# Softmax denominators of the attention stage: block transposes and sums on VectorE with two 16-column products, in place of two 512-column products

## The chip, the cores and the metric

The kernel runs on one core of a Trainium2 chip. A core has TensorE (PE in the rows; its weight loads are shown apart, as PEld), VectorE (DVE), ScalarE (ACT), GpSimd (POOL) and SyncE (SP, which issues most DMAs). Each engine runs its own instructions strictly in order, and engines wait for each other through semaphores. The metric is the device time of one execution in microseconds; lower is better.

## The reference

A block of four residual layers on x of 4 sequences x 1024 tokens x 256 features: a head-mixing layer, an expert layer (8 experts, 256 tokens of each sequence for each), causal attention with 16 heads of 64, and the expert layer again. The change lies in the attention:

```python
q = einsum('ntc,hdc->nhtd', x_q, w_q)        # likewise k, v
a = einsum('nhtd,nhsd->nhts', q, k) / sqrt(64)
a = where(causal_forbidden, -inf, a)
a = softmax(a, axis=3)                        # exp(a - max) / sum over s
y = einsum('nhts,nhsd->nthd', a, v).reshape(n, t, -1)
return y @ w_o
```

The changed part computes the sum over s for each head and query, takes its reciprocal, and brings it into the layout in which the values' product is multiplied by it.

## The kernel before

**Stages by time.** Head mixing and the first expert layer fill the span up to about 605 us, the attention runs to about 1800 us (its first unit overlaps the end of the first expert layer), and the second expert layer takes the rest.

**Units, chunks, pairs.** Attention is done in 32 units: 4 sequences x 8 head pairs, the two heads of a pair side by side in every tile. A unit has two chunks of 512 queries. Chunk 0 uses key blocks 0 to 3 (of 128 keys), chunk 1 key blocks 0 to 7. Key blocks go two at a time, so a unit has 6 such steps: two for chunk 0 and four for chunk 1. A step writes scores with keys on the partitions (L1423, L1439), ScalarE takes the exponential into a tile t_p of 128 keys x 2 heads x 512 queries (L1734), GpSimd masks the diagonal blocks (L2410) and adds the tiles of a chunk into t_acc (L2427, L2430), and TensorE multiplies the values by t_p into bank 6 (L1458, `weigh`). ScalarE copies the finished chunk to t_pvs (L1752).

**Denominators.** t_acc holds sums over key blocks; the sum over its 128 partitions is still to be taken. `divide` does it on TensorE (L1468): for each head a product of 64 columns of ones with 512 columns of t_acc, which leaves the sum repeated on 64 partitions. `sum_rows` on VectorE transposes the bank in 32x32 blocks (L2239) and takes the reciprocal of one column of 32 (L2241); `scale_rows` transposes back a 32-fold repeated copy (L2248) into t_den; GpSimd multiplies t_pvs by it into t_yT (L2444), from which the output product L1483 is made.

**Maxima of the next unit.** While a unit is attended, TensorE makes score rows of the next one (L1388, 512 columns; L1401, 128 or 256 columns) and VectorE takes their maxima (L2215 with the mask, always followed by a read of the accumulator, and L2221). After the last of them TensorE turns the 16x128 maxima (L1410, `max_rows`), VectorE negates them (L2230, t_neg), and a DMA moves them into a row of t_qb. The first score product L1439 of the next unit waits for that DMA. TensorE also makes the projections of the unit after (L1360, L1374), whose rests VectorE takes (L2199, L2185).

**What sets the order.** A hand-written set of Python generators, run once per engine. `attend` gives 24 places per unit, and the loop of `units` hangs the other work on places by number. `finish(n)`, run after the scores of step n, issues `divide` of a chunk three steps after its last pair started, then the weigh of the step before, then `sum_rows`, and `scale_rows` one step later. Seven banks of PSUM (0 to 5 and 7) are handed out in rotation, in TensorE's order, to scores, maxima, projections and denominators. A bank can be written again only when its reader has drained it, so the taker of a bank waits for the reader of whatever took it seven takes before.

## Time and profile before

| | |
|---|---|
| median of 3 runs | 2219.75 us (2218.33 to 2220.87) |
| the profiled execution | 2221.76 us, its span 2220.0 us |
| TensorE busy | 2142.3 us (97%) |
| VectorE busy | 1463.3 us (66%) |
| GpSimd busy | 1374.8 us (62%) |
| ScalarE busy | 1002.8 us (45%) |
| granted TensorE clock, mean | 0.989 |
| chain that ended last | TensorE 74%, VectorE 8%, GpSimd 4%, issue 3% |

The span runs from the first to the last instruction. The busy share of TensorE counts the time in which at least one matmul is in flight, and the starts of matmuls that follow each other without a wait are closer together than their durations, since they are pipelined. So what a group of matmuls costs is read as the distance from its first start to the start of the next group. The times at the left of the timeline rows below are such starts.

### The profile page before, as it was taken

How to read it: one execution, taken by the hardware profiler on the slowest of the kernel's cores; microseconds unless marked ns; L12 is line 12 of the kernel's file. 1: busy time of each engine (PE TensorE's matmuls, PEld its weight loads, DVE VectorE, ACT ScalarE, POOL GpSimd, SP SyncE). 2: the span in 40 equal slices, each digit the busy share in tenths (PEclk: the TensorE clock that was granted, in tenths of full speed). 3: DMA queues.
4: the chain of work that ended last, by engine and by line, in shares of the span. 5: the costliest groups of instructions: out<-in, count | busy, mean ns of one | idle time of the engine just before them, and what ended most of it. 6: DMA issues, size and time to landing. Idle time of an engine off the chain costs nothing.

```text
span 2220.0 us, 34078 instructions
## 1 busy us (share of the span) xinstructions
PE 2142.3 (97%) x12130; PEld 1597.7 (72%) x12130; DVE 1463.3 (66%) x3344; ACT 1002.8 (45%) x1908; POOL 1374.8 (62%) x1242
## 2 busy tenths in 40 slices
PE   7998999999999999999999999999999999999997
PEld 5446888889876666766667666567666588899997
DVE  7375687776757666476775577874876646975553
ACT  6302543454355555255553355542555425444442
POOL 4313675777357676466664566663777846777774
PEclk9999999999999999999999999999999899999999
DMA  4524554555432221221222132222221245545552
GB/s 133 185 95 127 140 134 103 142 141 134 98 92 58 58 58 49 67 77 51 75 70 74 39 86 50 56 67 64 61 77 30 67 135 130 139 111 132 136 143 29
DMA packets 145048, 206.04 MB, mean 93 GB/s; under 512 B 19432, under 2 KB 112112, under 8 KB 144880
## 3 DMA queue, kind: packets, MB, share of 16 engines
q1 hardware_dynamic: 120304, 170.30, 25.7%
q0 software_dynamic: 24576, 33.57, 9.1%
q8 instruction: 97, 1.59, 0.3%
q14 instruction: 71, 0.58, 0.1%
HBM read 130.03 MB, written 39.85 MB: 77 GB/s over the span
## 4 chain that ended last, share of the span: by engine, by line
PE 74%; DVE 8%; POOL 4%; issue 3%; ACT 2%; DMA 1%; SPq 1%; POOLq 0%; DVEq 0%; ACTq 0%
PE psum L1311 12%; PE psum L1332 11%; PE psum L1458 11%; PE psum L1360 8%; PE psum L1423 7%; PE psum L1439 6%; PE psum L1483 5%; PE psum L1374 4%; PE psum L1388 3%; PE psum L1468 3%; POOL t_acc L2430 2%; DVE f_hlo L2169 1%; DVE f_hhi L2167 1%; PE psum L1401 1%; PE psum L1279 1%
## 5 line engine op out<-in xcount | busy, mean ns | idle before, releaser
L1734 ACT ACTIVATE t_p<-psum 128x512 f32<-128x512 f32 (+3 forms) x768 | 323.6, 492 | 294.1 <-PE psum L1439 285.8
L2430 POOL TENSOR_TENSOR t_acc<-t_acc,t_p 128x1024 f32<-128x1024 f32 (+3 forms) x256 | 417.0, 1629 | 14.5 <-ACT t_p L1734 0.5
L2349 POOL TENSOR_TENSOR f_wlo<-f_wst,f_whi 128x256 fp32r<-128x256 f32 x256 | 222.1, 944 | 149.8 <-ACT f_whi L1667 149.8
L1332 PE MATMUL psum<-f_whi,f_hhi 128*128 128x256 f32 x1024 | 295.4, 288 | 7.9 <-DVE f_hlo L2169 7.8
L1458 PE MATMUL psum<-t_p,t_v 128*64 128x512 f32 (+3 forms) x1536 | 289.1, 497 | 5.0 <-POOL t_p L2410 5.0
L1332 PE MATMUL psum<-f_whi,f_hlo 128*128 128x256 f32 x1024 | 289.9, 283 | 0.0
L1332 PE MATMUL psum<-f_wlo,f_hhi 128*128 128x256 f32 x1024 | 289.7, 283 | 0.0
L2167 DVE CAST f_hhi<-f_h 128x512 fp32r<-128x512 f32 x256 | 141.2, 552 | 207.0 <-ACT f_h L1685 206.2
L1685 ACT ACTIVATE f_h<-psum 128x512 f32<-128x512 f32 x256 | 153.0, 598 | 275.6 <-PE psum L1311 263.1
L1423 PE MATMUL psum<-t_qa,t_ka 128*128 128x512 f32 (+3 forms) x768 | 224.3, 372 | 1.8 <-DVE t_mx L2215 0.8
L2430 POOL TENSOR_TENSOR t_acc<-t_p 128x768 f32<-128x768 f32 x64 | 134.5, 2102 | 137.0 <-PE psum L1468 133.7
L1458 PEld LDWEIGHTS psum<-t_p,t_v 128*64 128x64 f32 x1536 | 99.2, 137 | 159.4 <-issue 141.3
L2410 POOL TENSOR_SCALAR_AFFINE_SELECT t_p<-t_p 128x256 f32<-128x256 f32 x256 | 105.0, 420 | 174.8 <-ACT t_p L1734 174.1
L1439 PE MATMUL psum<-t_qb,t_kb 65*128 65x512 f32 (+3 forms) x768 | 207.3, 352 | 4.8 <-DMA t_qb<-t_neg 4.4
L1311 PE MATMUL psum<-f_xhi,f_whi 128*128 128x512 f32 x512 | 204.8, 400 | 7.0 <-DVE f_xlo L2153 3.8
L1332 PEld LDWEIGHTS psum<-f_whi,f_hhi 128*128 128x128 f32 x1024 | 195.3, 191 | 16.7 <-DVE f_hlo L2169 9.6
L2169 DVE TENSOR_TENSOR f_hlo<-f_h,f_hhi 128x512 fp32r<-128x512 f32 x256 | 199.7, 780 | 8.8
L1311 PE MATMUL psum<-f_xlo,f_whi 128*128 128x512 f32 x512 | 202.1, 395 | 0.0
L1311 PE MATMUL psum<-f_xhi,f_wlo 128*128 128x512 f32 x512 | 201.0, 393 | 0.0
L1332 PEld LDWEIGHTS psum<-f_wlo,f_hhi 128*128 128x128 f32 x1024 | 195.4, 191 | 4.8
L1332 PEld LDWEIGHTS psum<-f_whi,f_hlo 128*128 128x128 f32 x1024 | 195.3, 191 | 0.0
L2221 DVE TENSOR_REDUCE t_mx<-psum 128x1 f32<-128x512 f32 x256 | 159.6, 683 | 41.5 <-PE psum L1388 38.9
(291 smaller groups left out, 4401.6 us busy)
## 6 DMA issues: line engine op xcount, KB each, us to landing
f_wst<-in_L_ffn_w SPq DMA_DIRECT2D x64, 1024.0 KB, 5.5
t_ka<-t_ka SPq DMA_DIRECT2D x64, 256.0 KB, 3.5
t_qb<-t_qa SPq DMA_DIRECT2D x64, 256.0 KB, 3.8
t_wk<-wkT SPq DMA_DIRECT2D x32, 256.0 KB, 4.1
t_wq<-wqT SPq DMA_DIRECT2D x32, 256.0 KB, 4.0
t_wv<-wvT SPq DMA_DIRECT2D x16, 512.0 KB, 4.7
normal<-f_xy SPq DMA_DIRECT2D x5, 1024.0 KB, 5.6
a_x<-in_L_attn_a_x SPq DMA_DIRECT2D x4, 1024.0 KB, 7.8
```

Of the source, the lines that this page charges most:

```text
L1311: m = pe.matmul(k.bank[b], w[:, dt, fs], x[:, dt, :], start=(dt == 0 and j == 0), stop=(dt == k.DT - 1 and j == 2))
L1332: m = pe.matmul(out, h[:, js], w[:, f, :], start=(f == 0 and a == 0 and j % 2 == 0), stop=(f == FT - 1 and a == 2), skip_group_check=True)
L1360: m = pe.matmul(k.bank[bank], w[:, part, ct, :], x[:, ct, cs], start=(ct == 0 and a == 0), stop=(ct == 1 and a == 2))
L1423: pe.matmul(k.bank[bank][:, q0:], hd["ka"][:, ks], hd["qa"][:, qs], start=True, stop=False)
L1439: pe.matmul(k.bank[banks[i]][:, q0:], hd["kb"][0:k.QROWS, ks], hd["qb"][0:k.QROWS, qs], start=False, stop=True).then_inc(k.filled[banks[i] ...
L1458: m = pe.matmul(k.bank[6][i * DH:(i + 1) * DH, q0:BANK], v[:, kt, vs:vs + DH], p[:, i, q0:BANK], start=(kt == 0), stop=(kt == last), skip_ ...
L1734: act.activation(p[:, i, q0:], k.bank[bank][:, q0:], ACT.Exp, scale=1.0 / float(np.sqrt(k.DH))).then_inc(k.drained[bank], 1)
L2167: dve.tensor_copy(hhi[:], h[:]).then_inc(k.d_h.sem, 1)
L2169: dve.tensor_tensor(hlo[:], h[:], hhi[:].bitcast(F32), ALU.subtract).then_inc(k.d_h.sem, 1)
L2221: s = dve.tensor_reduce(mx1[:, i, n - k.KPC:n - k.KPC + 1], part, AX.X, ALU.max)
L2349: m = pool.tensor_tensor(t["wlo"][n % 2][:, i, ks], t["wst"][:, i, ks], t["whi"][n % 2][:, i, ks].bitcast(F32), ALU.subtract)
L2430: pool.tensor_tensor(acc[:, :, q0:], (p0 if kt == 1 else acc)[:, :, q0:], p[:, :, q0:], ALU.add).then_inc(k.p_acc, 1)
```

## The change

The sum over partitions is split. For each chunk VectorE transposes t_acc itself in 32x32 blocks (128x1024, both heads; L2256 of the changed kernel) and sums each run of 32 columns (L2258), which leaves `part`, 128 x 32 (16 columns for each head): at partition 32g+b, column n, the sum over the 32 partitions of quadrant g for query 32n+b. TensorE then adds the four quadrants with a constant `fold`, which has a one where the partition and the output row agree modulo 32: two products with 64 columns of weights and 16 moving columns (L1482), in place of two with 512 moving columns. VectorE takes the reciprocal straight from the bank (L2265, 128x16) and transposes the repeated copy as before (L2271). The transposed 128x1024 tile and the two final denominator tiles share their memory, so `fold_sums` waits until GpSimd has made the multiplication of the chunk before. GpSimd's first addition into t_acc of a chunk now waits for the transposition of the chunk one unit back, not for the product.

Chunk 0 is folded at place 19 of its unit, behind the last maxima of the next unit, and divided at the first place of the next unit. Chunk 1 is folded at the start of step 2 of the next unit and divided at step 3. Two reductions of 128x32 build `fold` in the constants.

```diff
-        self.d_den = Marks(s("dve_den"), "reciprocal", "rows")
+        self.d_den = Marks(s("dve_den"), "turned", "part", "rows")
...
+        self.fold = c("fold", [P, self.DH])
...
-        t["den"] = [sb("t_den", [P, BANK]) for _ in range(2)]
+        t["turned"] = sb("t_turned", [P, 2 * BANK])
+        t["den"] = [t["turned"][:, c * BANK:(c + 1) * BANK] for c in range(2)]
+        t["part"] = sb("t_part", [P, 2 * BANK // 32])
...
+        def fold(n):
+
+            if ends(n - 3) and pairs[n - 3][1]:
+                self.fold_sums(*pairs[n - 3][:2])
+
         def finish(n):
 
-            if ends(n - 3):
-                self.divide(*pairs[n - 3][:2])
+            done = [pairs[n - 5 + c][:2] for c in range(NC) if ends(n - 5 + c) and pairs[n - 5 + c][1] == c]
+            for u, c in done:
+                self.divide(u, c)
+                self.sum_rows(u, c)
             if 0 < n <= len(pairs):
                 u, c, kt = pairs[n - 1]
                 self.weigh(u, c, kt)
                 self.weigh(u, c, kt + 1)
-            if ends(n - 3):
-                self.sum_rows(*pairs[n - 3][:2])
-            if ends(n - 4):
-                scale(*pairs[n - 4][:2])
+            for u, c in done:
+                scale(u, c)
...
+                fold(n)
                 sums(n, 0)
...
+                    if place == 19:
+                        self.fold_sums(u, 0)
...
             for n in range(4):
+                fold(len(pairs) + n)
                 sums(len(pairs) + n, 0, 1)
...
     def divide(self, u, c):
...
-        self.wait_ge(k.p_acc, k.sum_count(u, c, k.KPC * (c + 1) - 1))
+        self.wait_ge(k.d_den.sem, k.d_den.at(2 * u + c, "part"))
         for i in range(2):
-            m = pe.matmul(k.bank[bank][i * DH:(i + 1) * DH, :], k.ones[:, 0:DH], t["acc"][(2 * u + c) % 2][:, i, :],
+            m = pe.matmul(k.bank[bank][i * DH:(i + 1) * DH, 0:n], k.fold[:], t["part"][:, i * n:(i + 1) * n],
                           start=True, stop=True, skip_group_check=True)
...
+        for n in range(0, k.DH, 32):
+            dve.tensor_reduce(k.fold[:, n:n + 32], k.ident[:].rearrange("p (g d) -> p d g", d=32), AX.X, ALU.add)
...
+    def fold_sums(self, u, c):
+
+        k, dve, t = self.k, self.e, self.k.t
+        chunk = 2 * u + c
+        self.wait_ge(k.p_acc, k.sum_count(u, c, k.KPC * (c + 1) - 1))
+        if chunk:
+            self.wait_ge(k.p_yt, chunk)
+            self.wait_filled(("den", (chunk - 1) // 2, (chunk - 1) % 2))
+        dve.transpose(t["turned"][:], t["acc"][c][:].rearrange("p i q -> p (i q)")).then_inc(k.d_den.sem, 1)
+        self.wait_ge(k.d_den.sem, k.d_den.at(chunk, "turned"))
+        dve.tensor_reduce(t["part"][:], t["turned"][:].rearrange("p (n j) -> p n j", j=32), AX.X,
+                          ALU.add).then_inc(k.d_den.sem, 1)
+
     def sum_rows(self, u, c):
...
-        dve.transpose(den[:], k.bank[bank]).then_inc(k.drained[bank], 1)
-        self.wait_drained(("den", u, c))
-        dve.reciprocal(t["rden"][chunk % 2][:, :], den[:].rearrange("p (n j) -> p n j", j=32)[:, :, 0]
-                       ).then_inc(k.d_den.sem, 1)
+        dve.reciprocal(t["rden"][chunk % 2][:, :], k.bank[bank][:, 0:BANK // 32]).then_inc(k.drained[bank], 1)
...
-                self.wait_filled(("den", u - 1, c))
+                self.wait_ge(k.d_den.sem, k.d_den.at(2 * (u - 1) + c, "turned"))
```

**TensorE, from the last projection of a unit into the next unit's first step.** L1360 is a projection, L1410 the turning of the maxima, L1458 the values' product, L1423 a score product. Before:

```order
L1360 MATMUL psum<-t_xThi,t_wk 128x512 x2
L1360 MATMUL psum<-t_xTlo,t_wk 128x512
L1410 MATMUL psum<-ident,t_mx 16x128
L1458 MATMUL psum<-t_p,t_v 64x256 x2
L1458 MATMUL psum<-t_p,t_v 64x128 x2
L1423 MATMUL psum<-t_qa,t_ka 128x512 x2
```

Of the change (the same instructions have line numbers 13 higher; L1482 is the new product):

```order
L1373 MATMUL psum<-t_xThi,t_wk 128x512 x2
L1373 MATMUL psum<-t_xTlo,t_wk 128x512
L1423 MATMUL psum<-ident,t_mx 16x128
L1482 MATMUL psum<-t_part,fold 64x16 x2
L1471 MATMUL psum<-t_p,t_v 64x256 x2
L1471 MATMUL psum<-t_p,t_v 64x128 x2
L1436 MATMUL psum<-t_qa,t_ka 128x512 x2
```

The product of chunk 0 used to stand two steps earlier, some 35 rows ahead of this piece counting single matmuls; it now stands directly behind the turning of the maxima.

**VectorE, from the last maximum of the next unit to the first rest of a projection.** Before (L2215 is a masked maximum and its read, L2248 the last transposition of chunk 0, L2230 the negation, L2199 the rest):

```order
L2215 ISA psum,t_mx<-psum,t_mask,t_mx_142 128x512
L2215 ISA t_mx 128x1
L2248 STREAM_TRANSPOSE t_den<-t_rden 128x512
L2230 TENSOR_SCALAR t_neg<-psum 16x128
L2199 TENSOR_TENSOR t_kb<-psum,t_ka 64x512 x2
```

Of the change (L2231 is the masked maximum, L2246 the negation, L2215 the rest):

```order
L2231 ISA psum,t_mx<-psum,t_mask,t_mx_143 128x512
L2231 ISA t_mx 128x1
L2256 STREAM_TRANSPOSE t_turned<-t_acc 128x1024
L2258 TENSOR_REDUCE t_part<-t_turned 128x32
L2246 TENSOR_SCALAR t_neg<-psum 16x128
L2265 RECIPROCAL t_rden<-psum 128x16
L2271 STREAM_TRANSPOSE t_turned<-t_rden 128x512
L2215 TENSOR_TENSOR t_kb<-psum,t_ka 64x512 x2
```

Ahead of the negation one 128x512 transposition is replaced by a 128x1024 transposition and a 128x1024 sum, and a reciprocal and the transposition now stand behind it.

**VectorE, the short masked maxima of the next unit.** Before:

```order
L2215 ISA psum,t_mx<-psum,t_mask 128x256
L2215 ISA t_mx 128x1
L2239 STREAM_TRANSPOSE t_den<-psum 128x512
L2241 RECIPROCAL t_rden<-t_den 128x16
L2221 TENSOR_REDUCE t_mx_142<-psum 128x1 x4
```

Of the change:

```order
L2231 ISA psum,t_mx<-psum,t_mask 128x512
L2231 ISA t_mx 128x1
L2256 STREAM_TRANSPOSE t_turned<-t_acc 128x1024
L2258 TENSOR_REDUCE t_part<-t_turned 128x32
L2231 ISA psum,t_mx<-psum,t_mask 128x128
```

The fold of chunk 1 stands four maxima earlier than the transposition that it replaces, ahead of the maxima of 128 and 256 columns.

## Rows read from the trace of the kernel before

**Rows 1.** The page: busy time of each engine, share of the span, instructions.

```profile
PE 2142.3 (97%) x12130; PEld 1597.7 (72%) x12130; DVE 1463.3 (66%) x3344; ACT 1002.8 (45%) x1908; POOL 1374.8 (62%) x1242
```

**Rows 2.** Stretch of the attention: length, busy time by engine, PEclk, DMA share, GB/s.

```profile
650.00:1740.00 1090.00, 1081.55 (x5870) 714.21 (x5866) 743.61 (x1934) 529.90 (x1129) 702.81 (x640) 1.00 0.22 60
```

**Rows 3.** TensorE's waits, 650 to 1740 us: releaser, total us, times, longest.

```profile
PE psum L1439 <- DMA t_qb<-t_neg: 4.4, 2, 2.2
PE psum L1423 <- DVE t_mx L2215: 0.8, 3, 0.3
```

**Rows 4.** Groups by shape: busy us, mean ns of one, idle before, releaser.

```profile
L1468 PE MATMUL psum<-t_acc,ones 128*64 128x512 f32 x256 | 69.1, 618 | 0.1
L2239 DVE STREAM_TRANSPOSE t_den<-psum 128x512 f32<-128x512 f32 x64 | 45.9, 717 | 35.0 <-PE psum L1468 31.6
L2248 DVE STREAM_TRANSPOSE t_den<-t_rden 128x512 f32<-128x512 f32 x64 | 45.0, 703 | 0.0
L2011 DVE TENSOR_SCALAR_CACHE_REDUCE e_junk<-e_pT,e_thr 128x1024 bf16<-128x1024 f32 x9 | 11.4, 1272 | 0.1
L2241 DVE RECIPROCAL t_rden<-t_den 128x16 f32<-128x16 f32 x64 | 16.2, 254 | 2.2
L2022 DVE STREAM_TRANSPOSE f_turned<-f_ind 128x32 f32<-128x32 f32 x30 | 6.4, 212 | 1.0
L2116 DVE TENSOR_REDUCE f_R<-f_junk 128x32 f32<-128x256 f32 x6 | 3.7, 610 | 0.2
```

**Rows 5.** Timeline of a plain unit, TensorE and VectorE: start, length, engine, line.

```profile
778.59 1.08 PE L1468 MATMUL psum<-t_acc,ones 128*64 128x512 f32 x4
779.50 1.89 PE L1458 MATMUL psum<-t_p,t_v 128*64 128x512 f32 x8
...
784.21 0.14 DVE L2215 DVE_READ_ACCUMULATOR2_ANT t_mx<- 128x1 f32 x1
784.21 0.71 DVE L2248 STREAM_TRANSPOSE t_den<-t_rden 128x512 f32<-128x512 f32 x1
...
786.16 0.27 PE L1410 MATMUL psum<-ident,t_mx 128*16 128x128 f32 x1
786.36 0.87 PE L1458 MATMUL psum<-t_p,t_v 128*64 128x256 f32 x8
786.47 0.28 DVE L2230 TENSOR_SCALAR t_neg<-psum 16x128 fp32r<-16x128 f32 x1 [1.54 <-PE psum L1410]
```

**Rows 6.** Timeline: two short products of known size, each with what starts next.

```profile
1015.75 1.03 PEld L1233 LDWEIGHTS psum<-f_gateT,e_yT 128*128 128x128 f32 x8
1016.81 0.30 PEld L1360 LDWEIGHTS psum<-t_xThi,t_wq 128*128 128x128 f32 x2
...
1115.09 0.44 PE L1458 MATMUL psum<-t_p,t_v 128*64 128x128 f32 x4 [0.43 <-POOL t_p L2410]
1115.46 0.73 PE L1423 MATMUL psum<-t_qa,t_ka 128*128 128x512 f32 x2
```

**Rows 7.** Timeline of a unit with a norm in VectorE's order, around the negation.

```profile
1111.86 0.14 DVE L2215 DVE_READ_ACCUMULATOR2_ANT t_mx<- 128x1 f32 x1
1117.55 0.24 DVE L2230 TENSOR_SCALAR t_neg<-psum 16x128 fp32r<-16x128 f32 x1
1119.78 0.47 PE L1439 MATMUL psum<-t_qb,t_kb 65*128 65x512 f32 x1 [2.21 <-DMA t_qb<-t_neg]
```

**Rows 8.** Timeline: the 128-column maxima in a plain unit (766) and a tight one.

```profile
766.30 0.14 DVE L2215 DVE_READ_ACCUMULATOR2_ANT t_mx<- 128x1 f32 x1
768.26 0.30 DVE L2215 CUSTOM_DVE_ANT_0 psum<-psum,t_mask 128x128 f32<-128x128 f32 x1 [1.82 <-PE psum L1401]
...
830.99 0.33 DVE L2215 CUSTOM_DVE_ANT_0 psum<-psum,t_mask 128x128 f32<-128x128 f32 x1
...
832.85 0.73 PE L1388 MATMUL psum<-t_ka,t_qa 64*128 64x512 f32 x4
```

**Rows 9.** Timeline of the last unit's start: GpSimd's masks, a VectorE product, TensorE.

```profile
1739.83 3.08 POOL L2410 TENSOR_SCALAR_AFFINE_SELECT t_p<-t_p 128x256 f32<-128x256 f32 x2
1740.30 1.20 DVE L2082 TENSOR_TENSOR e_A<-e_hi,iota 128x1024 f32<-128x1024 int32 x1
1742.96 0.69 PE L1458 MATMUL psum<-t_p,t_v 128*64 128x128 f32 x4 [2.02 <-POOL t_p L2410]
1746.66 2.30 DVE L2082 TENSOR_TENSOR e_A<-e_hi,iota 128x1024 f32<-128x1024 int32 x1
1779.50 0.67 PE L1483 MATMUL psum<-t_wo,t_yT 128*128 128x256 f32 x2 [1.94 <-POOL t_yT L2444]
```

More of the change, by code:

```diff
@@ L420 @@
     xt_block = qk_load = v_load = qk_product = qk_low = qk_double = v_product = skip
-    row_max = part_max = max_rows = high_scores = scores = weigh = add_up = divide = sum_rows = scale_rows = skip
+    row_max = part_max = max_rows = high_scores = scores = weigh = add_up = skip
+    fold_sums = divide = sum_rows = scale_rows = skip
     values_done = out_weights = out_load = out_product = out_add = skip
@@ L1464, in divide @@
         DH = k.DH
+        n = BANK // 32
         bank = self.take(("den", u, c), self.work_bank())
-        self.wait_ge(k.p_acc, k.sum_count(u, c, k.KPC * (c + 1) - 1))
+        self.wait_ge(k.d_den.sem, k.d_den.at(2 * u + c, "part"))
         for i in range(2):
-            m = pe.matmul(k.bank[bank][i * DH:(i + 1) * DH, :], k.ones[:, 0:DH], t["acc"][(2 * u + c) % 2][:, i, :],
+            m = pe.matmul(k.bank[bank][i * DH:(i + 1) * DH, 0:n], k.fold[:], t["part"][:, i * n:(i + 1) * n],
                           start=True, stop=True, skip_group_check=True)
@@ L2235, in sum_rows @@
         bank = self.wait_filled(("den", u, c))
-        den = t["den"][c]
-        if chunk > 1:
-            self.wait_ge(k.p_yt, chunk - 1)
-        dve.transpose(den[:], k.bank[bank]).then_inc(k.drained[bank], 1)
-        self.wait_drained(("den", u, c))
-        dve.reciprocal(t["rden"][chunk % 2][:, :], den[:].rearrange("p (n j) -> p n j", j=32)[:, :, 0]
-                       ).then_inc(k.d_den.sem, 1)
+        dve.reciprocal(t["rden"][chunk % 2][:, :], k.bank[bank][:, 0:BANK // 32]).then_inc(k.drained[bank], 1)
     def scale_rows(self, u, c):
@@ L2246, in scale_rows @@
         chunk = 2 * u + c
-        self.wait_ge(k.d_den.sem, k.d_den.at(chunk, "reciprocal"))
-        dve.transpose(t["den"][c][:], spread(t["rden"][chunk % 2][:], 2, 32)).then_inc(k.d_den.sem, 1)
+        self.wait_drained(("den", u, c))
+        dve.transpose(t["den"][c], spread(t["rden"][chunk % 2][:], 2, 32)).then_inc(k.d_den.sem, 1)
     def out_add(self, b, c, n):
@@ L2443, in scale_rows @@
         self.wait_ge(k.a_pvs, chunk + 1)
-        pool.tensor_tensor(t["yT"][c][:, hp, :], t["pvs"][chunk % 2][:], t["den"][c][:],
+        pool.tensor_tensor(t["yT"][c][:, hp, :], t["pvs"][chunk % 2][:], t["den"][c],
                            ALU.mult).then_inc(k.p_yt, 1)
```

## The prediction

> **What bounds the kernel now.** I read the page's busy times first: TensorE is busy 97% of the span, VectorE 66%, GpSimd 62% [rows 1]. The second view is the windows. In the attention, 650 to 1740 us, TensorE is busy 1081.6 of 1090 us at the full granted clock, 1.00, which is the 2.4 GHz level; VectorE is busy 743.6 us, 68% [rows 2]. The third view is TensorE's list of waits in that stretch. It waits 4.4 us in two pieces for the DMA of the negated maxima, 0.8 us for VectorE's maxima, and little else [rows 3]. So the attention is bound by how many columns TensorE streams. What is taken from it comes off the time, unless the change makes it wait, and there is next to no waiting now that could absorb anything. VectorE's and GpSimd's idle time costs nothing, which includes GpSimd's long wait for the old product.
>
> **1. Two products of 512 columns go.** Rows of a group overlap, so the cost is the distance between starts: the denominator product starts at 778.59 and the next product at 779.50, 0.91 us [rows 5]. That is done for 64 chunks: 64 x 0.91 = 58.2 us. (The group's busy time, 69.1 us [rows 4], counts the overlap with the next product.) All of it is on the path.
>
> **2. Two products of 16 columns come.** The trace has none with 64 columns of weights and 16 moving. Four records with 64-column weights and 128 moving columns, half of the eight of the last two key blocks, take 1115.46 - 1115.09 = 0.37 us; eight records with full weights and 8 moving columns take 1016.81 - 1015.75 = 1.06 us, so four take 0.53 [rows 6]. Below, four records cannot take less than a fourth of the 0.53, say 0.13. With half the weights of the second and an eighth of the columns of the first I take 0.30, nearest to the first: 64 x 0.30 = 19.2 us, with ends of 8 and 34 us. The page "TensorE: Matmul & The Clock Gate" of the Trainium skill, section LDWEIGHTS, gives a weight load as its columns divided by 1.2, in ns; an estimate from it is 53 ns for 64 columns, 0.21 us for four, and the sum would then be 5.8 us lower. The rows do not show a load of that size standing alone.
>
> **3. What a fold costs on VectorE.** A transposition of 128x512 takes 703 ns and one of 128x32 takes 212 ns [rows 4], so a column costs 1.02 ns and 1024 columns 1.23 us. The sum of 1024 columns into 32: a pass over 128x1024 with an accumulated sum takes 1.27 us, a sum of 256 columns, read with a stride, into 32 takes 0.61 us, four times that is 2.4 [rows 4]. Here the columns lie side by side, so I take 1.30. With 0.03 between them a fold is 2.56 us; the ends are 2.3 and 3.7. In return a 0.72 us transposition goes, and the reciprocal of 16 columns stays at about 0.25 [rows 4]. VectorE gains about 1.8 us of work a chunk, 118 us in all, and rises from 68% to near 81% in the attention. That alone does not bind; where the folds stand does.
>
> **4. The product of chunk 0 waits for its fold.** This is a new wait, in a place with little room. In a plain unit the last masked maximum ends for VectorE's next instruction at 784.21, and TensorE reaches the place of the new product at 786.36 [rows 5], 2.15 us later. The last maximum itself follows TensorE's score rows, so both move up together when an earlier product goes, and the distance stays. The fold is ready at 784.21 + 2.56 + 0.08 for the semaphore = 786.85: TensorE waits 0.49 us. Behind it stand the values' products and the first scores of the next unit. I counted the distance at all 32 negations: 22 units have this one (2.0 us from the end of the read), 3 have sequence-end products in between (8.5), 5 have transpositions or a short gate product between, and two at the ends lie otherwise. So 22 x 0.49 = 10.8 us. At a fold of 2.3 it would be 5 us, at 3.7 it would be 36.
>
> **5. The negation comes later.** VectorE now does 2.56 us ahead of it in place of 0.70, while TensorE is 0.49 + 0.30 later. In a plain unit the negation then starts at 786.8, 0.3 us later than now, and the scores that wait for it 0.8 later, so nothing is lost. In the units in which a norm also stands ahead of it, there is a wait already: negation at 1117.55, score product at 1119.78 after 2.21 us of waiting [rows 7]. There 1.86 - 0.79 = 1.07 us is added, twice, and about 0.4 in one more: 2.5 us.
>
> **6. The fold of chunk 1 holds up the short maxima.** In a plain unit VectorE is idle from 766.44 to 768.26 at this place [rows 8], and the fold ends at about 769.0. The maxima of 128 columns are 0.7 late, and TensorE takes their bank again seven takes later, with the fourth of the wide maxima, some 1.7 us after they are drained. Nothing is lost. Where VectorE has no gap, as at 830.99, with the wide rows only 1.86 us behind [rows 8], the masked maxima drain at 834.2 while TensorE wants the bank at about 832.3 (832.85, 0.5 to the fourth, less 0.91 and with waits of the pair before): 1.9 us, and about 0.3 more behind it. Four units are like that (the ones without value projections), 8.8 us. Four with a norm there lose about 0.6 each, the first unit 1.1, one more 0.2: 12.5 us together, with ends of 0 and 25, since one bank later or earlier decides.
>
> **7. The end.** GpSimd's multiplication of chunk 0 moves behind one more addition, which the first output product already waits 1.94 us for; that costs up to 1.3. Against it, the first VectorE products of the last unit start some 2 us later, so GpSimd's two masks, 3.08 us now, may get through before them, and a wait of 2.02 us of TensorE shrinks [rows 9]. I take 0, with ends of -4 and +2. The two reductions that build the constant lie ahead of the first load's arrival.
>
> **Sum.** -58.2 + 19.2 + 10.8 + 2.5 + 12.5 + 0 = -13.2 us. The profiled execution took 2221.76 us, span 2220.0 and 1.8 around it; it would become 2208.6. The median is 2.0 us lower, 2219.75, so I forecast 2206.5.
>
> **Rivals.**
>
> A. *Folds hide altogether* (both are short enough, or banks leave more room): terms 4 to 6 vanish and 39 us remain, 2181 us. For it speaks that VectorE has 32% idle. Against it, the 2.15 us in front of the product is less than two passes over 1024 columns can take. A partial form, a fold of 2.3 and no loss in term 6, gives -26, 2194.
>
> B. *The fold is slow, and the kernel becomes slower.* One mechanism: the sum runs at the strided rate, 2.4 us, so a fold takes 3.7. Term 4 becomes 22 x 1.63 = 36, term 5 rises by 1.1 in about 6 units to 9, term 6 by 1.1 in the 9 tight units to 22: -58 + 19 + 36 + 9 + 22 = +28, 2248 us. The point from which it turns is a fold of 2.56 + 13.2/37 = 2.92 us, with 37 places that pay. A lesser cause of the same wait is GpSimd: a VectorE product of 1024 columns took 1.20 us at 1740.30 but 2.30 us at 1746.66 beside GpSimd [rows 9], while accumulated passes kept to 1.27 [rows 4]. The Trainium skill, "SBUF — State Buffer", section Who interferes with whom, says that a VectorE instruction with at most one SBUF input and outside the two-port modes does not contend with GpSimd; both instructions of the fold have one, so by that rule this does not happen here, and the two rows agree.
>
> C. *The gain goes back into waits.* VectorE at 81% has backlogs that carry from the fold of chunk 1 through the wide maxima to the last one, so that each of some 10 tight units loses another 1.3 us, half of a fold: 13 us, no change, 2220.
>
> **How the numbers follow.** The forecast's mechanism, net gain with both waits, gets 0.66 (2196 to 2215 as its own range), A with its partial form 0.10, C 0.13, B 0.11. A change under 0.2%, 4.4 us, cannot be told from none here. Faster takes the forecast's and A's: 0.74, since a little of the forecast's upper tail is in "same" but C's spreads to both sides; same 0.14; slower 0.12. The range runs from 2191, where the fold is short and the small products cost 0.2, to 2223, a fold of 3.0.
>
> **What would show it.** L1482: 256 records, 0.3 us from first start to what follows. L2256 near 1.23 and L2258 near 1.30 us, whatever GpSimd does. TensorE's waits: VectorE's part or an unnamed issue in front of L1482 at chunk 0, about 0.5 us in some 22 units; waits on maxima, L2231 and L2237, in the four units near 831, 1131, 1433 and 1724; L1452 on the DMA near 3.3 us twice. GpSimd's 133 us wait in front of t_acc shrinks without any effect. Wrong would be: a fold far from 2.56 us, TensorE waiting at chunk 1's product, or an attention that shortens by less than 5 us with no such waits.

## The result: the changed kernel is not faster

| | before | after |
|---|---|---|
| median of 6 runs each, one chip | 2219.91 us | 2225.72 us (2220.9 to 2231.84) |
| ratio, 95% interval | | 1.0023 (1.0013 to 1.0033) |
| profiled execution, its span | 2221.76, 2220.0 us | 2225.34, 2223.6 us |
| granted TensorE clock, mean | 0.989 | 0.981 |

The forecast was 2206.5 us and its range ended at 2223, so it was wrong in sign: 5.8 us slower instead of 13 us faster. Where I give the ratio of a run below in microseconds, it is the ratio times 2220.6 us, because the chips differ.

**The profile after.** The page first, the row that answers to [rows 1]:

```profile
PE 2118.9 (95%) x12130; PEld 1595.9 (72%) x12130; DVE 1566.4 (70%) x3410; ACT 1003.1 (45%) x1908; POOL 1377.0 (62%) x1242
```

TensorE does 23 us less in a span that is 3.6 us longer. In the attention, the stretch of [rows 2], its idle time rose from 8.5 to 34.1 of 1090 us and the granted clock fell from 1.00 to 0.98:

```profile
650.00:1740.00 1090.00, 1055.87 (x5852) 710.18 (x5849) 834.52 (x1986) 529.45 (x1126) 700.50 (x639) 0.98 0.22 60
```

TensorE's waits in the same stretch (total us, times, longest), to be held against [rows 3]:

```profile
PE psum L1401 <- DVE t_mx L2231: 9.1, 8, 1.9
PE psum L1452 <- DMA t_qb<-t_neg: 8.0, 10, 2.2
PE psum L1482 <- DVE t_part L2258: 7.2, 22, 0.3
PE psum L1471 <- POOL t_p L2433: 4.9, 3, 2.1
```

L1482 is the new small product, L1401 are the score rows, L1452 the score product that needs the negation. The groups by shape (busy us, mean ns of one, idle before):

```profile
L2256 DVE STREAM_TRANSPOSE t_turned<-t_acc 128x1024 f32<-128x1024 f32 x64 | 79.3, 1240 | 5.2 <-POOL t_yT L2467 4.2 <-POOL t_acc L2453 1.0
L2258 DVE TENSOR_REDUCE t_part<-t_turned 128x32 f32<-128x1024 f32 x64 | 78.1, 1220 | 2.2
L1482 PE MATMUL psum<-t_part,fold 128*64 128x16 f32 x256 | 19.2, 222 | 9.5 <-DVE t_part L2258 9.0 <-DVE t_xTlo L2201 0.5
```

A fold takes 2.46 us, as forecast within 0.1, and its two instructions take 1.23 to 1.25 and 1.22 us in all 64 places, whatever GpSimd was doing.

**A plain unit**, timeline (start, length, engine, line), the end of a unit as in [rows 5]:

```profile
748.96 1.24 DVE L2256 STREAM_TRANSPOSE t_turned<-t_acc 128x1024 f32<-128x1024 f32 x1
750.24 1.22 DVE L2258 TENSOR_REDUCE t_part<-t_turned 128x32 f32<-128x1024 f32 x1
751.51 0.30 PE L1482 MATMUL psum<-t_part,fold 128*64 128x16 f32 x4 [0.33 <-DVE t_part L2258]
751.65 0.85 PE L1471 MATMUL psum<-t_p,t_v 128*64 128x256 f32 x8
```

The product of chunk 0 waits 0.33 us, and the next product starts 0.14 us behind its start. Such units became 1.1 us shorter (negation to negation: unit 3 from 32.34 to 31.25). The loss is in others. **Unit 14** has no value projections, and the fold of the chunk before stands right in front of the short maxima:

```profile
1122.41 1.24 DVE L2256 STREAM_TRANSPOSE t_turned<-t_acc 128x1024 f32<-128x1024 f32 x1
1123.25 0.49 PE L1401 MATMUL psum<-t_ka,t_qa 64*128 64x512 f32 x2
1123.68 1.22 DVE L2258 TENSOR_REDUCE t_part<-t_turned 128x32 f32<-128x1024 f32 x1
1124.82 0.29 DVE L2231 CUSTOM_DVE_ANT_0 psum<-psum,t_mask 128x128 f32<-128x128 f32 x1
...
1125.56 0.50 PE L1401 MATMUL psum<-t_ka,t_qa 64*128 64x512 f32 x2 [1.81 <-DVE t_mx L2231]
1125.98 1.22 PE L1436 MATMUL psum<-t_qa,t_ka 128*128 128x512 f32 x2
```

TensorE wants the bank of the 128-column maxima at 1123.74 and gets it at 1125.56. Then comes what I had not priced: two products of 512 columns (L1436) last 1.22 us, where the same pair takes 0.73 at 1119.62. The windows show why; the last three numbers of a row are PEclk, DMA share and GB/s:

```profile
1120.00:1124.00 4.00, 3.72 (x22) 2.37 (x20) 3.93 (x11) 2.75 (x5) 3.06 (x4) 1.00 0.90 245
1124.00:1126.00 2.00, 0.44 (x3) 0.23 (x3) 2.00 (x8) 0.01 (x1) 2.00 (x1) 1.00 0.04 11
1126.00:1128.00 2.00, 2.00 (x8) 1.63 (x6) 2.00 (x6) 0.28 (x1) 0.13 (x1) 0.50 0.00 0
1128.00:1130.00 2.00, 2.00 (x7) 1.27 (x5) 1.11 (x5) 0.95 (x3) 0.00 (x0) 0.50 0.00 0
1130.00:1132.00 2.00, 2.00 (x9) 0.75 (x10) 0.97 (x2) 0.94 (x2) 0.35 (x1) 0.50 0.01 4
```

TensorE is busy 0.44 of the 2 us from 1124, and from 1126 to 1132 the granted clock is 0.50, the 1.2 GHz level. Between 600 and 1820 us the clock records give 54.6 us at that level, 23.9 in the kernel before.

**The late negation** (L2246), here in a unit with a norm (L1844), to be held against [rows 7]:

```profile
1609.81 1.22 DVE L2258 TENSOR_REDUCE t_part<-t_turned 128x32 f32<-128x1024 f32 x1
1610.94 3.17 DVE L1844 TENSOR_SCALAR t_xy<-t_xy,t_mv,t_rstd 128x256 f32<-128x256 f32 x2
1614.04 0.27 DVE L2246 TENSOR_SCALAR t_neg<-psum 16x128 fp32r<-16x128 f32 x1
1616.31 0.70 PE L1452 MATMUL psum<-t_qb,t_kb 65*128 65x512 f32 x2 [2.22 <-DMA t_qb<-t_neg]
```

The fold and 3.17 us of norm stand ahead of the negation, and the score product that needs it waits 2.22 us. The kernel before has no such wait in this unit.

**The last unit**, against [rows 9]:

```profile
1744.67 0.30 PE L1482 MATMUL psum<-t_part,fold 128*64 128x16 f32 x4 [1.82 <-DVE t_part L2258]
1782.26 1.19 PE L1497 MATMUL psum<-t_wo,t_yT 128*128 128x256 f32 x2 [4.32 <-POOL t_yT L2467]
```

**The account** of units 0 to 30 (negation to negation, after less before: +4.2 us): TensorE's idle time +27.2; half of the 30.7 us more at the lower clock (37.5 against 6.8 in these units), +15.4; the rest, -38.4, is left for the products' saving. That rest is a remainder and not a measurement: the same account of the tiny folds below, which have the same products, leaves -42.8, so some 4 us stand in neither term. A half is what a stretch at half the clock costs while TensorE is busy throughout; the experiments below give 0.42 and 0.53.

### The profile page after: what moved, and what is told of

Read it like the earlier page. It is cut to its first block, busy times and chain, and to the rows that moved or that the text cites. A ratio compares the mean times of both kernels' runs of the same rounds, so it can differ in the third digit from the quotient of the medians.

```text
span 2223.6 us, 34020 instructions
## 1 busy us (share of the span) xinstructions
PE 2118.9 (95%) x12130; PEld 1595.9 (72%) x12130; DVE 1566.4 (70%) x3410; ACT 1003.1 (45%) x1908; POOL 1377.0 (62%) x1242
## 4 chain that ended last, share of the span: by engine, by line
PE 62%; DVE 13%; issue 6%; POOL 5%; ACT 3%; DMA 1%; SPq 1%; POOLq 0%; DVEq 0%; ACTq 0%
PE psum L1324 12%; PE psum L1345 11%; PE psum L1471 8%; PE psum L1436 5%; PE psum L1373 5%; PE psum L1497 5%; PE psum L1452 4%; PE psum L1387 4%; PE psum L1401 3%; POOL t_acc L2453 2%; DVE psum L2231 2%; DVE f_hlo L2185 1%; DVE t_turned L2256 1%; DVE f_hhi L2183 1%; PE psum L1414 1%
## 5 line engine op out<-in xcount | busy, mean ns | idle before, releaser
L1471 PE MATMUL psum<-t_p,t_v 128*64 128x512 f32 (+3 forms) x1536 | 295.2, 505 | 6.4 <-POOL t_p L2433 6.4
L1436 PE MATMUL psum<-t_qa,t_ka 128*128 128x512 f32 (+3 forms) x768 | 227.8, 376 | 2.1 <-DVE t_kb L2215 0.6
L1452 PE MATMUL psum<-t_qb,t_kb 65*128 65x512 f32 (+3 forms) x768 | 209.0, 354 | 8.6 <-DMA t_qb<-t_neg 8.5
L1471 PEld LDWEIGHTS psum<-t_p,t_v 128*64 128x64 f32 x1536 | 94.5, 138 | 119.3 <-issue 94.9
```

Source lines behind the costliest of these rows:

```text
L1436: pe.matmul(k.bank[bank][:, q0:], hd["ka"][:, ks], hd["qa"][:, qs], start=True, stop=False)
L1452: pe.matmul(k.bank[banks[i]][:, q0:], hd["kb"][0:k.QROWS, ks], hd["qb"][0:k.QROWS, qs], start=False, stop=True).then_inc(k.filled[banks[i] ...
L1471: m = pe.matmul(k.bank[6][i * DH:(i + 1) * DH, q0:BANK], v[:, kt, vs:vs + DH], p[:, i, q0:BANK], start=(kt == 0), stop=(kt == last), skip_ ...
```

## The experiments

In the diffs, `folded(u, c)` tells which chunks take the new way; the others keep the two 512-column products and the transposition of 128x512 at the places of the kernel before. Each ratio compares runs of the two kernels on one chip. Units 5, 13, 21 and 29 are those with u % 8 == 5: the fold of their chunk 1 stands in the next unit, so in the four tight units 6, 14, 22 and 30. The changes of length of single units tell most, so they stand together here (us, negation to negation, against the kernel before; unit 3 is a plain one):

| unit | after | tiny folds | chunk 1 only | without u % 8 == 5 | chunk 1 with zero products | chunk 0 split, without u % 8 == 5 |
|---|---|---|---|---|---|---|
| 3 | -1.09 | -1.47 | -0.74 | -0.73 | -0.74 | -1.49 |
| 6 | +1.18 | -1.46 | +1.20 | +0.02 | +1.20 | -0.73 |
| 14 | +2.96 | -1.56 | +5.72 | -0.90 | +1.06 | -2.22 |
| 22 | +3.50 | -1.21 | +5.23 | +1.38 | +2.66 | -1.85 |
| 30 | +5.38 | -1.48 | +1.18 | 0.00 | +1.17 | -0.38 |

### How long a fold may be: tiny, half and long folds

The plus lines belong to three kernels and are shortened; in the first two the sum is cut to the same columns.

```diff
-        dve.transpose(t["turned"][:], t["acc"][c][:].rearrange(...))
+        dve.transpose(t["turned"][:, 0:32], t["acc"][c][:, 0, 0:32])      # tiny
+        dve.transpose(t["turned"][:, 0:BANK], t["acc"][c][:, 0, :])       # half
+        dve.tensor_reduce(t["spare"][:], t["turned"][:]..., ALU.max)      # long: added
```

> The changed kernel with the VectorE work of every fold cut from a 128x1024 transpose and a 1024-element sum (1.23 + 1.22 us) to a 32-column transpose and the sum of 32 columns (about 0.1 us each); all waits, products and their order stay. It leaves out the sums over the partitions, so the denominators are not the softmax's. Theory (the 39 us that the smaller products save on TensorE are eaten by waits behind the folds, 27 us of idle gaps more than before, and by about 31 us more at the lower clock, which those gaps bring): the gaps and the stretches at the lower clock go back to what the kernel before had or less, and the time is 2176 to 2190 us, about 40 below the changed kernel. Rival 1 (the new small products and what is queued around them on TensorE cost more than their rows show): the time stays within 10 us of the changed kernel, 2216 or more. Rival 2 (the place of the first chunk's product in the next unit costs by itself): about half of the gain, 2200 to 2210.

Measured: 2181.15 us, ratio 0.9821 (0.9808 to 0.9833). Between 600 and 1820 us it has 20.5 us at the lower clock. That is the theory's case, and both rivals fall.

> The changed kernel with each fold over one head's 512 columns alone (0.65 + 0.62 us by half of the rows' durations), for both chunks; it leaves out the other head's sums. With folds of 0.26 us the time was 2181, with 2.46 us 2226. Theory (a unit can hide about 1 us of a fold, and each tenth more is waited for): 2183 to 2192. Rival (the cost is in proportion to the fold's length from the start): 2201, range 2197 to 2205.

Measured: 2190.74 us, ratio 0.9832 (0.9819 to 0.9846).

> The changed kernel with a second pass of 1.22 us over the turned sums in each fold (a maximum whose result is not used), so that a fold takes 3.7 us. Between folds of 1.25 us (36.8 us below the kernel before) and of 2.46 us (5.1 above) the time rose by 35 us per us of fold. Theory (each further tenth is waited for in all units): 42 us more than the changed kernel, a ratio of 1.021 (1.015 to 1.026). Rival (the waits of different kinds overlap, so that a longer fold costs only where it already costs): 1.010 or less.

Measured: 2273.45 us, ratio 1.0235 (1.0221 to 1.0249). The rows of the fold in the tiny and in the half kernel, then two of TensorE's waits in the long one, whose fold is three instructions of 1.24, 1.22 and 1.21 us (the line numbers shift by two or so):

```profile
L2258 DVE STREAM_TRANSPOSE t_turned<-t_acc 128x32 f32<-128x32 f32 x64 | 13.1, 205 | 5.5 <-POOL t_yT L2469 4.2 <-POOL t_acc L2455 1.3
L2260 DVE TENSOR_REDUCE t_part<-t_turned 128x1 f32<-128x32 f32 x64 | 11.9, 186 | 2.2
```

```profile
L2258 DVE STREAM_TRANSPOSE t_turned<-t_acc 128x512 f32<-128x512 f32 x64 | 45.2, 706 | 5.1 <-POOL t_yT L2469 4.2 <-POOL t_acc L2455 1.0
L2260 DVE TENSOR_REDUCE t_part<-t_turned 128x16 f32<-128x512 f32 x64 | 43.9, 686 | 2.2
```

```profile
PE psum L1483 <- DVE t_part L2260: 35.2, 25, 2.9
PE psum L1402 <- DVE t_mx L2232: 23.5, 16, 3.0
```

So against a kernel before of 2220.6 us: a fold of 0.39 us gives -39.7, 1.39 us -37.3, 2.46 us +5.1, 3.67 us +52.2. The first microsecond costs 2.4 us, the next 1.07 cost 42, the last 1.21 cost 47, with L1483 and L1402 (L1482 and L1401 of after) waiting 59 us. For the half fold the theory of a hidden first microsecond holds, for the long fold the theory that each further tenth is waited for. With the slope of the long fold the knee comes out near 1.4 us. My slope of 37 us for each microsecond of fold is near the 39 of the long one, but for another reason in part: of its 50.5 us more in units 0 to 30, 40.8 are idle time and 17.1 are at the lower clock, which my 37 places left out. Where the line begins I had wrong.

### Which chunk: chunk 1 alone, chunk 0 alone

```diff
+    def folded(self, u, c):
+        return c == 1          # chunk 0 alone: c == 0
```

> The first chunk's denominators by the method before (two 512-column products at the old places, one 128x512 transpose), the second chunk's by folds as in the changed kernel. Half of the products' saving is kept: about -19 us against the kernel before. Theory: the visible waits of the chunk-0 product (22 of about 0.33 us) and the late negations (8.5 us) go, the waits for the short maxima behind the chunk-1 folds stay (about 9 us, with some of the lower clock, 3 to 5 us): 2211 to 2217 us, faster than both. Rival (the second chunk's fold does the harm): 2220 or more.

> The second chunk's denominators by the method before, the first chunk's by the fold behind the unit's last maximum and the product in the next unit, as in the changed kernel. Theory: -19 us for the products, +7 us for the visible waits of the chunk-0 product, +8.5 us for the late negations, some 5 us for the lower clock behind them, nothing of the short maxima's waits: 2216 to 2223 us, so the worse half. Rival (the two halves are worth the same, the clock does the rest): equal to the kernel with the second chunk alone within 2 us.

Measured: chunk 1 alone 2215.89 us, ratio 0.9978 (0.9968 to 0.9988), inside the theory's range; chunk 0 alone 2231.68 us, 1.0049 (1.0036 to 1.0062). Chunk 0 is the worse half, but its time missed my range, which ended at 2223. Its waits for the negation are 9.4 us and for the fold 7.3, about as expected; GpSimd's masks add 4.9, and its units have 20.5 us more at the lower clock than the kernel before (27.3 against 6.8), about 10 us where I had put 5. -4.9 and +10.9 add up to +6.0, near the +5.1 of both. But chunk 1 alone is no plain gain: by the table, units 14 and 22 lose over 5 us, the same wait costs units 6 and 30 only +1.2.

### The place of chunk 0's fold

```diff
-                    if place == 19:
+                    if place == 17:
                         self.fold_sums(u, 0)
```

> The changed kernel with the fold of the first chunk two pairs earlier in VectorE's order, ahead of the last two masked maxima of the unit, and nothing else moved. Theory: the product of chunk 0 no longer waits (7 us), the negation is as late as the sum of the same instructions in the norm units, so at most half of its 8.5 us goes, and part of the lower clock with them: 2208 to 2216 us. Rival 1 (it is the amount of VectorE work ahead of the negation, not its order, that makes the units wait): the negation's waits stay, 2219 to 2224 us. Rival 2 (the fold now stands in front of the masked maxima, which the first scores of the next unit need, and GpSimd hasn't finished the chunk's sum): slower than the changed kernel, 2230 or more.

Measured: 2228.34 us, ratio 1.0027 (1.0017 to 1.0038), no different from after. The theory falls. At 2220.6 it is 2226.6 us, between the ranges of the two rivals; the waits show the second one's mechanism, with less weight:

```profile
PE psum L1436 <- DVE t_mx L2231: 24.9, 38, 0.9
PE psum L1401 <- DVE t_mx L2231: 9.0, 8, 1.9
PE psum L1452 <- DMA t_qb<-t_neg: 3.9, 3, 1.6
```

The wait of L1482 is gone and that of L1452 halved, but the masked maxima, now 2.46 us later, hold the banks of the last score products (L1436), 0.87 us in each plain unit. So next to each place stands something that can bear 1.2 us and not 2.5. That suggested cutting the fold in two:

```diff
+                    if place == 17:
+                        self.turn_sums(u, 0)       # the transposition
                     if place == 19:
-                        self.fold_sums(u, 0)
+                        self.part_sums(u, 0)       # the sum
```

> The changed kernel with the first chunk's fold in two pieces: its transpose (1.23 us) two pairs earlier, ahead of the masked maxima of 384 and 512 keys, where VectorE waits for TensorE, its sum (1.22 us) where it was. Theory (what costs is the length of uninterrupted VectorE work ahead of something that TensorE needs soon): the product of chunk 0 and the negation come 1.2 us earlier, the masked maxima are at most 0.3 us late; 2208 to 2216. Rival (the end of a unit has no spare time on VectorE at all, as the fold moved as a whole showed, so each piece is waited for somewhere): 2221 to 2229.

Measured: 2210.09 us, ratio 0.9921 (0.9907 to 0.9935), 17.5 us below the kernel before: the theory, and more than it expected. Unit 3 is 1.49 us shorter, as with tiny folds. What is left in the units are chunk 1's waits, eight of them as in the changed kernel, and the clock behind them (unit 6, whose wait of 1.65 us is as long as in the changed kernel, now has 6.8 us at the lower clock behind it and is +3.60 for +1.18):

```profile
PE psum L1403 <- DVE t_mx L2233: 9.0, 8, 1.9
PE psum L1454 <- DMA t_qb<-t_neg: 3.2, 2, 1.6
```

### Chunk 1 in the tight units

```diff
-        return c == 1
+        return c == 1 and hp != 5          # hp = u % 8
```

> The second chunk's denominators by folds as in the kernel with the second chunk alone (2215.9 us), but not in the four units of each batch's sixth pair of heads (u % 8 == 5), whose fold stands ahead of the short maxima of the units 6, 14, 22, 30; these four take the method before. Theory: those four units were 1.2, 5.7, 5.2 and 1.2 us longer than in the kernel before, by the wait for the short maxima and the lower clock behind it; now they are as before: 2215.9 - 13.3 = 2202.6, range 2200 to 2206. Rival (the wait only moves to another unit, or the clock falls there for another reason): 2212 or more.

Measured: 2211.47 us, ratio 0.9931 (0.9917 to 0.9944), which is 2205.3 at 2220.6: inside the range. Three of the four units lost their excess; in unit 22 6.8 us at the lower clock stayed behind another wait, that for the negation (+1.38).

```diff
-        return c == 1 and hp != 5
+        return c == 0 or hp != 5           # with chunk 0 in two pieces
```

> The kernel with the first chunk's fold in two pieces (ratio to the kernel before 0.9921), and the second chunk of the units u % 8 == 5 by the method before. Theory: what is left in the former are the units 6, 14, 22 and 30, 3.6, 3.5, 2.5 and 2.4 us longer than in the kernel before, behind the second chunk's fold; with the old method there they are 0.75 us shorter (one chunk's saving): 12 + 3 = 15 us less, a ratio of 0.9853 (0.984 to 0.987), or about 2188 us where the kernel before takes 2220. Rival (part of those waits is the price of the first chunk's fold, not the second's): a gain of under 8 us, 0.9885 or more.

Measured: 2187.62 us, ratio 0.9849 (0.9834 to 0.9864), as expected. Between 600 and 1820 us it has 13.7 us at the lower clock, less than the kernel before, and none in units 0 to 30.

Then both folds in two pieces, in all units; the transposition of chunk 1 stays where its fold stood:

```diff
+                    if place == 9 and u:
+                        self.part_sums(u - 1, 1)   # chunk 1's sum behind the short maxima
```

> Both chunks by folds in all units, each fold in two pieces: the first chunk's transpose two pairs earlier, the second chunk's sum two short maxima later (between them stand the short maxima that TensorE waits for). Theory (length of one uninterrupted stretch of VectorE work, not its sum, makes the waits): the units 6, 14, 22 and 30 have waits of about 0.6 us as with the folds of half the length, and gain what the others gain: a ratio of 0.983 to 0.986, near the 0.9821 of the kernel without folds. Rival (VectorE has no spare time for 2.46 us in these units, in whatever pieces): they stay 2 to 3.5 us longer than before, 0.991 to 0.993.

Measured: 2197.87 us, ratio 0.9894 (0.9879 to 0.9909), between the two. Unit 6 is +0.29, better than +1.2 but not the -0.6 of half folds, and every plain unit lost 0.47 us (unit 3: -1.02). The timeline of unit 3 shows it; L2301 is the sum, L2263 the wide maxima behind it:

```profile
735.28 1.21 DVE L2301 TENSOR_REDUCE t_part<-t_turned 128x32 f32<-128x1024 f32 x1
...
736.41 2.47 DVE L2263 TENSOR_REDUCE t_mx<-psum 128x1 f32<-128x512 f32 x4
...
737.15 1.10 PE L1455 MATMUL psum<-t_qa,t_ka 128*128 128x512 f32 x2
737.74 0.19 PEld L1455 LDWEIGHTS psum<-t_qa,t_ka 128*128 128x128 f32 x1 [0.41 <-DVE t_mx L2263]
```

In the tight units the cut helped; in the plain ones it moved a hidden sum into a place with no spare time. A piece must be short and stand where its neighbours have slack.

### The end

```diff
-        return True
+        return c == 1 or u < self.B * self.NHP - 1
```

> The same, but the first chunk of the very last unit by the method before, product and reciprocal in the unit itself. The wait of the last output product for GpSimd's product with the reciprocals was 1.94 us in the kernel before and 4.3 in the changed one, also in the one with folds of 0.26 us, and 1.9 where the first chunk keeps the old method. Theory (this wait is the price of the product's new place, which nothing hides in the last unit): 2.4 us less than the same kernel without this. Rival (the end is set by the second chunk's chain): no difference, within 0.7 us.

Measured: 2195.24 us, ratio 0.9881 (0.9866 to 0.9897), 2.6 us less by the medians. That agrees with the theory's 2.4; the intervals of the two ratios overlap, so by times alone it is not settled. The waits say the same again below.

### The clock

Seven zero products, first in front of a pair of 384 columns at place 6, then in front of the product that waits:

```diff
+            for a in range(k.idle):        # 7 in the units 6, 14, 22, 30
+                m = pe.matmul(k.bank[bank][:, 0:w]..., k.ones_b[:],
+                              spread(k.zeros[:], 1, w // 32), start=False, stop=a == k.idle - 1)
```

> The kernel with the second chunk's folds alone (2215.9 us), and ahead of the product that waits in the units 6, 14, 22, 30 seven products of 512 columns with zeros, added to the running weighted values, so that TensorE works in the wait of 1.8 us instead of standing. The wait itself stays. Theory (in units 14 and 22 the granted clock falls to 1.2 GHz behind this wait, for 13.7 and 10.2 us instead of 3.4, which makes them 4.5 and 4.0 us longer than units 6 and 30 with the same wait): the lower clock there goes back to 3.4 us and the time to 2207, range 2204 to 2210. Rival 1 (the clock there falls for something else than the wait): 2214 to 2218. Rival 2 (the zero products hold up what is behind them): 2218 or more.

Measured: 2215.35 us, ratio 0.9955 (0.9942 to 0.9969), but the run does not test what it was to test. In unit 14 the products ran at 1125.22, the product that waits came at 1131.80, and its wait was 0.70 instead of 1.50: they made TensorE later, so VectorE was less late. Units 6 and 30 became 0.9 us longer than with chunk 1 alone, units 14 and 22 became 5.3 and 3.9 us shorter, which can be the shorter wait or the clock. I repeated it at the right place.

> The kernel with the second chunk's folds alone (ratio to the kernel before 0.9978), and in the units 6, 14, 22, 30 seven products of 512 columns with zeros, this time right ahead of the product that waits (the first ones stood 5 us too early and shortened the wait instead of filling it). They are added to the second bank of the pair of score rows before, which VectorE takes later. The wait's end stays where it is, TensorE works until then. Theory (the granted clock falls behind TensorE's idle stretch, and that costs about 3 us in each of units 14 and 22, in excess of the wait): units 6 and 30 stay at +1.2 us, units 14 and 22 lose the stretch at 1.2 GHz behind the wait for the maxima: a ratio of 0.995 (0.9935 to 0.9965). Rival (the clock falls there whatever TensorE does in these 1.8 us): 0.9978, over 0.997.

> The changed kernel with the same zero products at the same place in the units 6, 14, 22, 30. Theory: the stretches at 1.2 GHz right behind the wait for the maxima go (6.8 us each in units 14, 22 and 30), those behind the late negation stay: 3 times 3 us less than the changed kernel, a ratio of 0.998 (0.997 to 0.9995) against 1.0023. Rival: 1.0023, over 1.001.

Measured: chunk 1 alone with zero products 2212.48 us, ratio 0.9939 (0.9926 to 0.9953), against 0.9978 without. The changed kernel with them 2220.88 us, 0.9977 (0.9968 to 0.9986), against 1.0023 (1.0013 to 1.0033). Both theories hold, and neither interval touches that of its kernel without. Unit 14 of the first, timeline and windows:

```profile
1128.54 0.50 PE L1417 MATMUL psum<-t_ka,t_qa 64*128 64x512 f32 x2
...
1128.98 1.68 PE L1422 MATMUL psum<-zeros,ones_b 128*128 128x512 bf16 x7
1130.59 0.50 PE L1417 MATMUL psum<-t_ka,t_qa 64*128 64x512 f32 x2
...
1132.24 0.68 PE L1459 MATMUL psum<-t_qa,t_ka 128*128 128x512 f32 x2
```

```profile
1125.00:1130.00 5.00, 5.00 (x31) 3.21 (x28) 4.93 (x12) 2.76 (x5) 3.67 (x4) 1.00 0.72 197
1130.00:1135.00 5.00, 5.00 (x28) 2.59 (x25) 4.92 (x18) 2.17 (x4) 1.14 (x1) 1.00 0.02 7
```

The same unit without them, in the kernel with chunk 1 alone:

```profile
1129.48 0.49 PE L1414 MATMUL psum<-t_ka,t_qa 64*128 64x512 f32 x2 [1.50 <-DVE t_mx L2251]
...
1131.41 1.16 PE L1449 MATMUL psum<-t_qa,t_ka 128*128 128x512 f32 x2
```

```profile
1130.00:1135.00 5.00, 5.00 (x18) 3.02 (x20) 4.00 (x12) 2.17 (x4) 0.17 (x2) 0.58 0.02 7
```

TensorE does 1.7 us of useless work, and the product behind it starts no earlier (2.05 us behind the one before it, 2.01 without). Yet the unit is 4.7 us shorter (+5.72 to +1.06), because the clock stays at 1.00, the 2.4 GHz level. Of the 10.3 us less at the lower clock in this unit (13.7 to 3.4), 6.8 lay behind the wait that was filled; the rest lay behind an earlier wait for the negation, which I did not touch, and which differed by itself. Units 6 and 30, which had no lower clock, are unchanged at +1.20 and +1.17. In the changed kernel units 14, 22 and 30 became 2.2, 3.2 and 3.0 us shorter, 8.5 together. Unit 11 became 1.5 us longer, with 3.4 us at the lower clock behind a wait for the negation of the same length as before. Units 0 to 30 together became 7.1 us shorter for 17.0 us less at the lower clock, 0.42 us for each; with chunk 1 alone they became 7.2 us shorter for 13.7 less, 0.53. The stretches behind the waits for the negation I did not test in this way. The Trainium skill, "TensorE: Matmul & The Clock Gate", section A second HAM failure mode: psum-queue depth-cycling, describes short idle times between groups of products as a cause of the clock going down and up, and the loss as that of throughput between the groups. In the two traces above the clock does fall behind the short idle time and not without it (0.58 against 1.00 from 1130 to 1135), and the loss lies in the products behind it: the same pair took 1.16 us instead of 0.68.

### The version that the runs point to

```diff
+        return c == 1 and hp != 5 or c == 0 and u < self.B * self.NHP - 1
```

> The first chunk by folds in two pieces (transpose two pairs earlier), but in the very last unit by the method before; the second chunk by folds in one piece, but in the units u % 8 == 5 by the method before. It joins the two edits that paid singly: 0.9849 without the last unit's exception, and 0.0013 for that exception. Theory (the two places are independent): a ratio of 0.9836 (0.982 to 0.985), 2184 us where the kernel before takes 2221. Rival (with the second chunk's transposes undivided the last unit is bound by the second chunk's chain, so the exception gives nothing here): 0.9849 (over 0.985).

Measured: 2183.52 us, ratio 0.9828 (0.9815 to 0.9841), 1.7% below the kernel before and 1.9% below the changed one. The output product's wait fell from 4.3 to 1.9 us (first row from the kernel without the last unit's exception, second with it):

```profile
PE psum L1519 <- POOL t_yT L2521: 4.3, 1, 4.3
```

```profile
PE psum L1519 <- POOL t_yT L2521: 1.9, 1, 1.9
```

```profile
650.00:1740.00 1090.00, 1071.64 (x6012) 721.64 (x6008) 846.76 (x2009) 543.95 (x1159) 736.18 (x663) 1.00 0.23 63
```

VectorE is busier in this stretch than in the changed kernel (846.8 against 834.5 us), and the clock is at 1.00. The two edits add up, and with 0.9821 for the tiny folds little of the folds is left to pay: 1.6 us, inside the intervals, and the 2.4 us at the end, which the tiny folds still pay.

## Why the prediction was wrong, by its own steps

**Steps 1 and 2, the products.** Right in kind, and better than forecast: the small products cost 0.14 us from their start to the next one's, the lower part of my 8 to 34 us (64 x 0.14 = 9, not 19.2). With tiny folds the whole change gives -39.7, 0.7 from my -39.0; that agreement is in part luck. It hides 10 us less for the small products and about as much lost elsewhere: units 0, 8, 16 and 24 became only 0.85 us shorter each where a plain unit became 1.47, and the end costs 2.4.

**Step 3, the fold.** 2.46 for 2.56 us. VectorE's busy time rose by 103 us for 118.

**Step 4.** 22 waits of 0.33 us, 7.2 us, for 22 of 0.49, 10.8. The count was exact.

**Step 5, the negation: too small.** The waits for its DMA went from 4.4 us in 2 pieces to 8.0 in 10, and two waits for GpSimd's masks took the place of the old ones (0.7 to 4.9 us): +7.8 us for 2.5. I had looked at the two units that waited already. The others with a norm in VectorE's order, such as the one at 1610.94, had had just enough slack.

**Step 6.** L1401 waits 9.1 us for 0.5, +8.6 for 12.5, in the units that I named.

**Steps 4 to 6 together** are 23.6 us of visible waits for a forecast of 25.8. The waits were not what made the forecast wrong.

**Step 7, the end.** 4.3 for 1.94 us at the output product (+2.4, the price that the last runs took away) and a chunk-0 wait of 1.8; against it the waits of 2.02 and 2.05 us for GpSimd's masks went down to one of 1.5. About +2 for 0.

**The step that failed** is a term that the sum puts at nothing. The argument starts from "at the full granted clock, 1.00", and nothing in the sum lets that clock fall behind the new waits. I priced every wait at its own length. The two traces differ by +3.6 us where the sum has -13.2; of these 16.8 us about 15 are the lower clock, worked out at a half of each microsecond (by medians the whole gap is 19.0). The trace before could have told me. Its two waits for the negation, 2.21 us at 1119.78 and 2.23 at 1420.60, are each followed by 3.4 us at the lower clock, which the mean of [rows 2] rounds away:

```profile
1121.60:1125.00 3.40, 3.40 (x14) 3.01 (x13) 1.65 (x4) 2.74 (x7) 1.42 (x3) 0.51 0.05 14
```

In the changed kernel seven of the nine waits of 1.6 us or more in units 0 to 30 are followed by such a stretch. Equal waits differ in this: 1.65 us in unit 30 brought 6.8 us at the lower clock, 1.65 us in unit 6 none. I cannot say from these traces what decides.

None of the signs that I had named as showing me wrong came: the fold was as long as forecast, TensorE did not wait at chunk 1's product, and the attention that did not shorten had the waits. The list had no sign for the clock.

**Rivals:** A was right on what is to be had (2181, 0.9821) and wrong on a whole fold hiding; half a fold does. Its partial form is mis-summed: with a fold of 2.3 us term 4 is 5 us and not 10.8, so without term 6 the sum is about -32 us, 2188, and not -26, 2194. B's fold length was not met, and when a fold of 3.67 us was built, it cost 52 us where B had 28. C named "no change" and the waits that take the gain; its time, 2220, was the nearest, though by its words the waits alone would do it.

## What to carry to other kernels

When work moves from the engine that sets the pace to one with idle time, price the longest uninterrupted piece of it at each place, not its sum: against pieces of 0.4 us, 1.4 us of VectorE work in one piece cost 2.4 us a kernel and 2.5 us in one piece cost 45, while the same 2.5 us in two pieces cost nothing in the plain units, where both places had slack. A wait of the pacing engine costs its length and perhaps as much again in the clock, so list the waits that a change adds and give the granted clock behind them a term of its own. Where a few units are tight, leave them on the old way rather than tune for all.

## What the hardware showed that I had not expected

- Behind TensorE's waits of 1.5 to 2.2 us the granted clock was 0.50 for 3.4 or 6.8 us, in some units and not in others; two products of 512 columns then took 1.16 to 1.22 us instead of 0.68 to 0.74. Zero products of 1.7 us in place of the wait for the maxima kept it at 1.00 there.
- Four small products (two of 64x16 in fp32, four records) hold TensorE for 0.14 us, though their records last 0.30.
- VectorE's sum of side-by-side columns took 0.19 us for 32 columns, 0.69 for 512 and 1.22 for 1024; the strided sum of [rows 4] had suggested up to twice that.
